# Turns spread over TensorE's order, a smaller ring of gathered rows, wider ids matmuls, and an earlier dense part in the last layer 1

## The reference

```python
e = jnp.stack([tbl_0[ids[:, 0]], ..., tbl_25[ids[:, 25]]], axis=1)      # 2048 x 26 x 128
combined = jnp.concatenate([e, r_dense_x[:, None, :]], axis=1)          # 27 vectors
interact = jnp.einsum('bfd,bgd->bfg', combined, combined)
z = interact[:, _TRIU_I, _TRIU_J]                                       # 351 products
h = jnp.concatenate([z, r_dense_x], axis=1)                             # 479
h = jnp.maximum(h @ W_top1 + b_top1, 0.0)                               # 512
h = jnp.maximum(h @ W_top2 + b_top2, 0.0)                               # 256
y = h @ W_top3                                                          # 1
```

## Time and profile before

| | us |
|---|---|
| median of three runs (412.57 to 418.06) | 412.77 |
| the profiled execution | 414.51 |
| its span in the trace | 412.7 |
| PE busy / weight loads | 382.2 / 355.1 |
| POOL busy | 283.1 |
| DVE busy | 246.2 |
| ACT busy | 236.7 |
| mean granted clock of TensorE | 0.979 |

### The profile page before, as it was taken

How to read it: one execution, slowest core, us unless ns; L and a number is a source line. 1 busy time by engine, 2 the same in 40 slices (tenths; PEclk the granted TensorE clock), 3 DMA queues, 4 the chain that set the end, 5 groups by cost and what they waited for, 6 DMA issues and landing times.

```text
span 412.7 us, 8012 instructions
## 1 busy us (share of the span) xinstructions
PE 382.2 (93%) x2976; PEld 355.1 (86%) x2976; DVE 246.2 (60%) x713; ACT 236.7 (57%) x429; POOL 283.1 (69%) x294
## 2 busy tenths in 40 slices
PE   5998989669896999999999999999999999999877
PEld 3888889558895999989999999989999999998766
DVE  6786988527584476827685667637683667133311
ACT  3467735625455465666656665665657655686334
POOL 6777777777777777777777777777777777771000
PEclk9999999959999899999999999999999999999989
DMA  8971231213212213222222223212222222211000
GB/s 210 262 230 51 52 94 54 67 46 89 66 54 68 65 52 85 65 63 68 71 68 69 66 57 85 72 53 64 76 69 67 65 68 70 70 55 49 6 14 2
DMA packets 21637, 30.54 MB, mean 74 GB/s; under 512 B 6960, under 2 KB 15864, under 8 KB 21472
## 3 DMA queue, kind: packets, MB, share of 16 engines
q0 software_dynamic: 9216, 18.89, 16.3%
q1 hardware_dynamic: 12041, 10.91, 10.1%
q10 hardware_dynamic: 343, 0.24, 0.2%
HBM read 26.86 MB, written 0.01 MB: 65 GB/s over the span
## 4 chain that ended last, share of the span: by engine, by line
PE 66%; POOL 22%; issue 7%; DMA 2%; ACT 1%; ACTq 1%; DVE 0%; POOLq 0%
POOL rows L263 22%; PE ps_gram L336 21%; PE ps_mlp L345 15%; PE ps_feat L315 10%; PE ps_feat L317 10%; PE ps_feat L279 6%; PE ps_feat L289 2%; DMA rows<-in_tbl,ids_now 2%; PE ps_mlp L411 2%; PE ps_mlp L352 1%; ACTq L202 1%; DMA ids_now<-in_ids_gathered 1%; PE ps_feat L352 1%; ACT hid L602 0%; POOLq L100 0%
## 5 line engine op out<-in xcount | busy, mean ns | idle before, releaser
L263 POOL DMA_INDIRECT rows<-in_tbl,ids_now x288 | 282.4, 981 | 89.2 <-issue 86.0
L761 DVE TENSOR_SCALAR hot<-ids_all,row_no 125x256 fp32r<-125x256 f32 x512 | 160.2, 385 | 6.0 <-ACT ids_all L558 2.9
L336 PE MATMUL ps_gram<-feat 128*123 128x108 f32 x1024 | 125.3, 278 | 3.3 <-ACT feat L524 3.3
L336 PEld LDWEIGHTS ps_gram<-feat 128*123 128x123 f32 x1024 | 118.2, 192 | 9.2 <-ACT feat L524 5.2
L315 PE MATMUL ps_feat<-hot,table_hi 125*128 125x256 f32 x480 | 117.8, 287 | 1.8 <-ACT stage L540 0.9
L317 PE MATMUL ps_feat<-hot,table_lo 125*128 125x256 f32 x480 | 115.5, 282 | 0.0
L510 DVE COPY z<-ps_gram 27x208 f32<-27x208 f32 x128 | 46.9, 366 | 105.3 <-PE ps_gram L336 102.1
L315 PEld LDWEIGHTS ps_feat<-hot,table_hi 125*128 125x128 f32 x480 | 90.5, 189 | 4.4 <-ACT feat L524 1.5
L317 PEld LDWEIGHTS ps_feat<-hot,table_lo 125*128 125x128 f32 x480 | 90.4, 188 | 0.0
L524 ACT COPY feat<-ps_feat 128x512 f32<-128x512 f32 (+1 forms) x80 | 76.6, 985 | 11.2 <-PE ps_feat L279 10.8
L510 ACT COPY z<-ps_gram 27x208 f32<-27x208 f32 x128 | 41.7, 326 | 55.2 <-PE ps_gram L336 53.5
(11 more groups left out here) (57 smaller groups left out, 319.4 us busy)
## 6 DMA issues: line engine op xcount, KB each, us to landing
rows<-in_tbl,ids_now POOLq DMA_INDIRECT x288, 2.5
table_lo_before<-in_tbl SPq DMA_DIRECT2D x8, 448.0 KB
dense<-in_dense_t SPq DMA_DIRECT2D x8, 128.0 KB
w_lo_before<-in_w SPq DMA_DIRECT2D x1, 1024.0 KB, 16.7
zp_lo_before<-in_dense_t SPq DMA_DIRECT2D x8, 128.0 KB, 2.5
zp_lo_before<-z SPq DMA_DIRECT2D x15, 39.0 KB
zp_lo_before<-z SPq DMA_DIRECT2D x15, 36.0 KB
w_lo_before<-in_w SPq DMA_DIRECT2D x1, 512.0 KB, 18.2
```

Source lines behind the costliest of these rows:

```text
L263: nc.gpsimd.indirect_dma_start(rows[:, row_at(t, f), :], None, gathered[f], bass.IndirectOffsetOnAxis(ap=ids_now[:, t, f:f + 1], axis=0),) ...
L336: mm = nc.tensor.matmul(ps_gram[at % 2][0:FOUR, c, 0:4 * F], four[:, 0:FOUR], four.rearrange("d (j f) -> d j f", f=FPAD)[:, :, 0:F], start ...
L761: op = nc.vector.tensor_scalar(hot[0:VROWS, u % HOTS, c, :], ids[0:VROWS, k, :], row_no[0:VROWS, no + UNIT * i + c:no + UNIT * i + c + 1], ...
```

## The change

Four edits. (1) The turns, the look-ups and the batches of products stand in another order in `even` and `odd`, on PE, ACT and DVE, and `feat_turns` counts them so. (2) The ring `rows` has 14 slots in place of 30. (3) `ids_few_no` and `ident_r` have 128 partitions, of which those from 4 on are zero in the first, and the ids matmul contracts over all. (4) At the end, the dense chunk of the last layer 1 is taken right after `layer1(6, 3)` and into other banks, and ACT and DVE make its operands, and the hidden part of half 6, before ACT issues its three packing DMAs; the store of y moves behind the last cast of `zp`.

```diff
-ROWS = GATHERED + 12
+ROWS = 14
...
-            order += [("tile", t, 0), ("pair", h, 2), ("tile", t, 1), ("ids", h + 1, 0), ("ids", h + 1, 1),
-                      ("pair", h, 3), ("tile", t, 2), ("tile", t, 3), ("tile", t, 4)]
+            order += [("tile", t, 0), ("pair", h, 2), ("tile", t, 1), ("ids", h + 1, 0), ("tile", t, 2),
+                      ("ids", h + 1, 1), ("pair", h, 3), ("tile", t, 3), ("tile", t, 4)]
...
-        ident, ident_r = sb("ident", [P, P]), sb("ident_r", [PAIRS, PAIRS], F32R)
+        ident, ident_r = sb("ident", [P, P]), sb("ident_r", [P, PAIRS], F32R)
-        ids_few_no = sb("ids_few_no", [PAIRS, 2, HALF], F32R)
+        ids_few_no = sb("ids_few_no", [P, 2, HALF], F32R)
...
+        last_gram = ps_gram[0][:].rearrange("p (i a) b -> p i (a b)", i=2)
-            return ps_feat[n - 2] if n in (2, 3) else ps_mlp[at % 2]
+            return ps_feat[n] if n in (0, 1) else last_gram[:, n - 2, :] if n in (2, 3) else ps_mlp[at % 2]
...
-                nc.tensor.matmul(ps_feat[at % 2][:], ident_r[:, p:p + 1].broadcast_to([PAIRS, P]),
+                nc.tensor.matmul(ps_feat[at % 2][:], ident_r[:, p:p + 1].broadcast_to([P, P]),
...
+            def last_layer1_dense():
+                h = HALVES - 1
+                pe.wait_ge(zp_lo_ready, h + 1)
+                pe.wait_ge(emptied, len(FEAT_AT))
+                for n in range(HID1 // P):
+                    if n == 2:
+                        pe.wait_ge(z_by_act, BATCHES * TILES - 1)
+                        pe.wait_ge(z_by_dve, BATCHES * TILES - 1)
+                    three(OUTS * h + n, w1_hi, w1_lo, zp_hi, zp_lo[h % 2], n, ZP_CHUNKS - 1, True, False)
...
@@ PE, odd(t)
-                turn(t, 1)
                 products(t - 1, 2)
+                turn(t, 1)
                 spread_ids(h + 1, 2)
                 products(t - 1, 3)
+                layer1(h - 2, 0)
+                turn(t, 2)
                 look_up(h + 1, 0)
-                turn(t, 2)
-                layer1(h - 2, 0)
+                layer1(h - 2, 1)
+                turn(t, 3)
                 spread_ids(h + 1, 3)
-                layer1(h - 2, 1)
+                layer1(h - 2, 2)
                 look_up(h + 1, 1)
-                turn(t, 3)
-                layer1(h - 2, 2)
                 turn(t, 4)
...
@@ PE, the end
             layer1(h, 3)
+            last_layer1_dense()
             layer2(h, 0)
...
@@ ACT, the end
+            act.wait_ge(packed_dense[(h + 1) % 2], 16 * ((h + 1) // 2 + 1))
+            act.wait_ge(mlp_done, OUTS * h + HID1 // P)
+            split_zp(h + 1, slice(ZP_CHUNKS - 1, ZP_CHUNKS))
+            result1(h, 3)
             pack_rects(act, TILES - 1, range(LAST_BY_SP, len(RECTS)))
-            result1(h, 3)
             result2(h, 0)
-            result2(h, 1)
-
-            act.wait_ge(packed_dense[(h + 1) % 2], 16 * ((h + 1) // 2 + 1))
-            split_zp(h + 1, slice(ZP_CHUNKS - 1, ZP_CHUNKS))
             zp_packed(TILES - 2)
             split_zp(h + 1, slice(0, ZP_CHUNKS - 1), slice(0, P))
-            store_y(h)
+            result2(h, 1)
             zp_packed(TILES - 1)
             split_zp(h + 1, slice(0, ZP_CHUNKS - 1), slice(P, HALF))
+            store_y(h)
...
@@ DVE, even(t)
                 take(t - 1, 2)
-                take(t - 1, 3)
                 put_dense(t)
                 build(h + 1, 0)
+                take(t - 1, 3)
                 rest_zp(h - 2)
...
+            nc.vector.memset(ids_few_no[:].bitcast(F32), 0.0).then_inc(constants_set, 1)
```

More of the change, by code:

```diff
@@ L69, in feat_turns @@
         if t % 2 == 0:
-            order += [("tile", t, 0), ("pair", h, 2), ("tile", t, 1), ("ids", h + 1, 0), ("ids", h + 1, 1),
-                      ("pair", h, 3), ("tile", t, 2), ("tile", t, 3), ("tile", t, 4)]
+            order += [("tile", t, 0), ("pair", h, 2), ("tile", t, 1), ("ids", h + 1, 0), ("tile", t, 2),
+                      ("ids", h + 1, 1), ("pair", h, 3), ("tile", t, 3), ("tile", t, 4)]
         elif h + 1 < HALVES:
-            order += [("tile", t, 0), ("tile", t, 1), ("ids", h + 1, 2), ("pair", h + 1, 0), ("tile", t, 2),
-                      ("ids", h + 1, 3), ("pair", h + 1, 1), ("tile", t, 3), ("tile", t, 4)]
+            order += [("tile", t, 0), ("tile", t, 1), ("ids", h + 1, 2), ("tile", t, 2), ("pair", h + 1, 0),
+                      ("tile", t, 3), ("ids", h + 1, 3), ("pair", h + 1, 1), ("tile", t, 4)]
         else:
@@ L370, in last_layer1 @@
                     for c in range(ZP_CHUNKS - 1):
-                        mm = three(at + n, w1_hi, w1_lo, zp_hi, zp_lo[h % 2], n, c, False, c == ZP_CHUNKS - 2)
+                        mm = three(OUTS * h + n, w1_hi, w1_lo, zp_hi, zp_lo[h % 2], n, c, False, c == ZP_CHUNKS - 2)
                     mm.then_inc(mlp_done, 1)
@@ L423, in even @@
                 spread_ids(h + 1, 0)
-                products(t - 1, 3)
+                turn(t, 2)
+                layer2(h - 3, 0)
                 spread_ids(h + 1, 1)
                 look_up(h, 3)
-                turn(t, 2)
-                layer2(h - 3, 0)
                 turn(t, 3)
+                products(t - 1, 3)
                 turn(t, 4)
@@ L438, in odd @@
                 layer3(h - 3)
+                products(t - 1, 2)
                 turn(t, 1)
-                products(t - 1, 2)
                 spread_ids(h + 1, 2)
                 products(t - 1, 3)
+                layer1(h - 2, 0)
+                turn(t, 2)
                 look_up(h + 1, 0)
-                turn(t, 2)
-                layer1(h - 2, 0)
+                layer1(h - 2, 1)
+                turn(t, 3)
                 spread_ids(h + 1, 3)
-                layer1(h - 2, 1)
+                layer1(h - 2, 2)
                 look_up(h + 1, 1)
-                turn(t, 3)
-                layer1(h - 2, 2)
                 turn(t, 4)
@@ L547, in number_ids @@
                     act.wait_ge(ids_spread, PAIRS * h)
-                copy(ids_few_no[:], ids_few[:]).then_inc(ids_few_ready, 1)
+                copy(ids_few_no[0:PAIRS, :, :], ids_few[:]).then_inc(ids_few_ready, 1)
             def empty_ids(h, p):
@@ L641, in odd @@
                 store_y(h - 3)
+                take(t - 1, 2)
                 empty_turn(t, 1)
-                take(t - 1, 2)
                 empty_ids(h + 1, 2)
@@ L839, in _ @@
             dve.wait_ge(ident_ready, 1)
-            copy(ident_r[:], ident[0:PAIRS, 0:PAIRS]).then_inc(ident_ready, 1)
+            copy(ident_r[:], ident[:, 0:PAIRS]).then_inc(ident_ready, 1)
             dve.wait_ge(row_no_ready, len(SIZES) + 1)
@@ L872, in _ @@
                 take(TILES - 1, b)
+            rest_zp(h + 1, 0, slice(ZP_CHUNKS - 1, ZP_CHUNKS))
             rest_hid1(h, 3)
-            rest_zp(h + 1, 0, slice(ZP_CHUNKS - 1, ZP_CHUNKS))
             rest_zp(h + 1, 1, slice(0, ZP_CHUNKS - 1), slice(0, P))
```

27 lines of the change are left out of this document (10 added, 17 removed).

## The result

The changed kernel took 409.17 us (median of seven runs, 406.50 to 409.70), the kernel before 412.77 in the same set (seven runs, 410.64 to 418.06): ratio 0.989, interval 0.985 to 0.994. It is about 1% faster, 3.6 us by the medians; the forecast was 410.7, 2.1 us less.

The account below looks back on a forecast made before the run. POOL alone was taken to fix when tile 15's second group lands, and so the end. Span 412.7 + 1.5 (collisions) - 3.6 (tail) = 410.6; on the median, 412.77 - 2.1 = 410.7 us, 8-in-10 range 406 to 416.

Parts of the forecast that it names:

- The signs: Whole kernel: wrong if POOL waits for turns, PE's half is longer than POOL's, or tile 15's group lands by 360.
- Turns spread, 0.3 us a half: PE's steady halves: the new order costs only bank waits, 0.3 us a half, bounds 0 and 4.2.
- Ids matmuls: PE's ids matmuls over 128 rows: 0.24 us instead of 0.42, saving 0.3 each, 1.2 a half, nothing at the end.
- the edit saves nothing: Rival on ids matmuls: weight loads cost by columns, not rows, so 128 rows save nothing; no chance of its own.
- Room for 14 rows: Ring of gathered rows: 14 slots cost 0, the tightest turn in the new order having 3.2 us to spare.
- Collisions, +1.5 us: POOL's gathers held up by DVE's subtractions before tile 15's second group: +1.5 us, bounds -2.6 and +5.6.
- The tail, -3.6: Kernel's end: dense part early, ACT's packing DMAs later, full clock; gain 3.6 us, bounds 1.9 and 4.0.
- the last is there at about 397.0: Tail: SP's issues end at 394.52, landing takes 2.3 to 3.6 us, so the last packing lands about 397.0.
- PE as the bound: Slower rival: ids matmuls keep 0.42 us and bank waits are real; 415.4 with w = 1.3; 9%.
- the fall of the clock: Rival in the tail: the clock falls all the same or a late landing holds PE; gain 1.9, 412.4; 11%.
- bad collisions: Rival: DVE's subtractions line up badly with POOL's gathers, +5.6 - 3.6, giving 414.8; 14%.
- the "faster" one: Rival: rest_zp falls between POOL's critical moments (-2.6) and the tail gives 4.0, so 406.2; 12%.

Follow-up runs that it names:

- e12: Changed kernel without the gathers of table 17 in the odd tiles (8 of 288 left out): 400.05 us against 413.16 for the kernel before, ratio 0.966.
- e3: Kernel before with only the new order of turns, look-ups and products on PE, ACT and DVE: 546.29 us, ratio 0.890.
- e2: Kernel before with only the ids matmuls widened to 128 rows: 600.53 us, ratio 0.981.
- e1: Kernel before with only the tail changed (last layer 1's dense part early, ACT's packing DMAs later): 610.05 us against 617.53, ratio 0.998.
- e9: Kernel before with four small memsets on POOL before each of the 80 groups of gathers, and 29 slots: 545.25 us against 620.23.
- the first pair: The first comparison, all four edits against the kernel before: 409.17 us against 412.77, ratio 0.989.
- e11: Changed kernel with four small memsets on POOL before each of the 80 groups of gathers: 480.97 us against 413.16 for the kernel before, ratio 1.162.

## Why the prediction was right, and where it wasn't

*The signs.* The prediction named three of being wrong, and two of them came. POOL waited for a turn, once, and the group of tile 15 landed at 358.60, earlier than 360 (in a trace that is the fastest of seven executions). The paragraphs on the room and on the collisions say what was wrong. The third, a half of PE longer than POOL's, didn't come (44.2 against 45.3). The main part of the last layer 1 begins 35.1 us after the landing, where 36 was forecast and 39.5 was before.

*The bound.* That POOL alone fixes the second group of tile 15, and this the end, is shown: pauses move it by +73.0, fewer gathers by -7.1, as POOL's own time goes. That PE turns from an equal into the one that waits is shown by the 12 waits and by e12.

*Turns spread, 0.3 us a half.* Right in that nothing of it reaches the end: PE has the room. Of the 0.3 us nothing is seen: in e12's two halves, which have this order, PE waits for no bank. It isn't shown alone where PE is supplied, because e3 ran where it was starved.

*Ids matmuls.* Forecast 0.24 us to the next work; the trace shows 0.32 (0.40 ahead of a look-up). Forecast 0.3 saved each and 1.2 a half; e2 shows 0.37 each among products, and PE's half is 1.2 shorter. The size held, though by another split: less in the step behind the matmul and more in the work around it. It was worth nothing at the end, as predicted. The weight load of an ids matmul takes 0.18 us with 4 rows and 0.19 with 128, so the rule of the Trainium skill (TensorE: Matmul & The Clock Gate, "LDWEIGHTS (loading the stationary operand)") stands as far as the load goes. What failed is the step from it to "the edit saves nothing": the saving isn't in the load.

*Room for 14 rows.* Predicted as free: POOL waited once, 0.84 us in place of the 0.30 of a gap, in tile 1, which the walk through the steady halves had passed over; in those halves not at all. As POOL alone sets the pace, these 0.5 us reach the end (e12 has the same wait).

*Collisions, +1.5 us.* The mis-sized term. In the profiled pair the excess over 0.945 us, of the gathers that took more than 0.98, fell from 10.0 to 6.3, -3.7, beyond my bound of -2.6. Of that the six `rest_zp` hold only 0.3 (1.6 to 1.25; one, at 350.58, has 0.5 of it). The rest came from the weights' split, 2.1 to 1.1, which I had at 1.7, and from the splits of the tables in the first 50 us, 4.3 to 2.6, which I had not counted at all; small ones make up the remaining 0.7. The weights' split and the last `rest_zp` in POOL's timeline, and below them that `rest_zp` on DVE (the first answers to 80.49 in the earlier trace rows, the second to 351.78):

```profile
81.71 2.06 POOL L265 DMA_INDIRECT rows<-in_tbl,ids_now  x1 [0.30 <-issue]
...
350.58 1.43 POOL L265 DMA_INDIRECT rows<-in_tbl,ids_now  x1 [0.30 <-issue]
...
349.97 1.22 DVE L754 TENSOR_TENSOR zp_lo<-zp_lo_before,zp_hi 128x1024 fp32r<-128x1024 f32 x1
```

But this is one execution of each. In e12, with the same DVE program, the splits have the same excess to 0.1 us (2.6 and 1.1), while the six `rest_zp` have 2.1 in place of 1.25: the early part repeats, the late one doesn't. I had taken 0.6 us as the mean of a `rest_zp`. In all three traces each gather that such a subtraction held up ended 0.82 us after the subtraction, so that the excess is at most about 1.0, and over all phases of the 1.25 us beat some 0.4 in the mean (an estimate), 2.3 for six.

By the medians the whole without the tail is -3.6 + 4.4 = +0.8, which has the sign of +1.5 and half its size; in the profiled pair it is -3.6. That the sum came near is therefore in part luck.

*The tail, -3.6.* -4.4, shown twice. The idle microsecond, the full clock and layer 2 in 2.9 us came as forecast (1.01, 1.00, 2.89). What failed is the step "the last is there at about 397.0": on the time axis of before, the last cast began at 392.54 + 3.56 = 396.1, 1.6 us after SP's last issue (390.95 in the changed kernel), so the landing took at most 1.6 from there and not 2.3 or more. I had counted the 2.3 us from the end of the last issue; from its start, 390.16, the cast is 2.38 away. With the packing early, layer 2 of half 6 and ACT's copy of it became last, and the gain went past my bound of 4.0. (The forecast's own terms, 397.0 + 0.51 + 0.57 + 0.12, give 398.2 and not 398.1.)

*The sum.* -2.1 forecast, -3.6 measured: 0.8 more from the tail, and 0.7 less lost in what stands before it, where collisions and the one wait can't be told apart by the medians. Of the rivals, PE as the bound, the fall of the clock and bad collisions did not come; the "faster" one was half right, in the tail.

*What I did not see at all* is the state in which PE is starved, and there the order of the turns, which I priced at 0.3 us a half, is worth 11%. Nothing in the trace of before showed it: POOL ran 288 gathers in one series, and PE's unexplained idle time was 0.9 us. Why PE is supplied on one chip and not on another stays open; the instruction queue q8 moved the same 24 packets in every trace.

## What to carry to other kernels

Find the one moment that fixes the end, and ask which engine fixes it; an edit to the other engine buys safety only, and a test that adds or removes a known piece of work settles it better than an argument. Where PE waits near the end of a kernel, moving ready work into the gap pays twice, for the gap and for the clock. A long unbroken series of gathers is a risk even where a profile shows it as free: the kernel whose order breaks it lost nothing when the chip was kind, and saved 14% when it wasn't (11% by the order alone).

## What the runs showed of the hardware

- On three of the chips PE idled for 32 to 104 us of a run with no semaphore to wait for. In e1 it started one matmul about every 1.0 us (0.12 otherwise) from the eighth gather of an unbroken series on; the granted clock fell with it, to 0.67 in the window of 210 to 225 us. With a pause before each group of gathers it was 45 us (e9) in place of 104 (e1). On the chips of the first pair and of e11 and e12 it was 0.0 to 0.9 us, with 288 gathers in a row too. No run shows why.
- Work behind an ids matmul of 512 columns starts after 0.32 us with 128 rows and after 0.42 with 4, and the matmul with 16 products behind it takes 1.95 and 2.32 us. The weight load takes 0.19 and 0.18.
- DVE's TENSOR_TENSOR holds up a gather until its own end, and the gather ends 0.82 us later (126.36 in the kernel before, 350.58 in the changed one). One that starts as the subtraction does isn't held up (34.72 in the changed kernel, 0.94 us). In e12 the excess is 0.3 to 0.9 us for a `rest_zp`. This agrees with the Trainium skill (SBUF — State Buffer, "SBUF: two separate sides"). TENSOR_SCALARs cost 0.1 us or less mostly, and up to 0.7 (222.38 in e12) now and then. They do 256 elements in 0.31 us, no faster for each element than a TENSOR_TENSOR (1024 in 1.22), so nothing here shows that they take two ports, as the prediction supposed.
